# Batch numbers read one unit ahead, first projection weights split early, five heads in halves, operands at 64 bytes

## The reference

```python
x = x + einsum('bct,bcd->bdt', x, W0[cond])                    # 16 maps of 32 x 32
x = x + einsum('bsi,boi->bso', x, W1[cond])                    # 16 maps of 512 x 512
x = x + einsum('bct,bcd->bdt', x, W2[subj]) + bias2[subj]      # 32 maps of 32 x 32
q, k, v = x @ Wq.T, x @ Wk.T, x @ Wv.T                         # 32 query heads, 8 key heads, D = 128
q, k = rope(rmsnorm(q)), rope(rmsnorm(k))
scores = q . [cached keys (16 pages of 32), new keys (32)]     # 4 query heads share a key head
probs = softmax(where(valid, scores * SCALE, -1e30))
x = x + (probs . [cached values, new values]) @ Wo.T
```

## Time and profile before

| | us |
|---|---|
| median of three runs | 2288.32 (2285.64 to 2289.05) |
| profiled execution, its own time | 2286.66 |
| its span in the trace | 2284.8 |

### The profile page before, as it was taken

How to read it: one execution, slowest core, us unless ns; L and a number is a source line. 1 busy time by engine, 2 the same in 40 slices (tenths; PEclk the granted TensorE clock), 3 DMA queues, 4 the chain that set the end, 5 groups by cost and what they waited for, 6 DMA issues and landing times. The chain is left out here.

```text
span 2284.8 us, 52315 instructions
## 1 busy us (share of the span) xinstructions
PE 2231.2 (98%) x16384; PEld 1935.1 (85%) x16384; DVE 1675.9 (73%) x3504; ACT 1297.7 (57%) x2643; POOL 1137.8 (50%) x1218
## 2 busy tenths in 40 slices
PE   7998999999998999999999999999999998999999
PEld 6777777777776999999999999999999997888887
DVE  7860788888887888888888888888888886422221
ACT  6732888888886555555555555555555555311111
POOL 5200354544445777777777777777777773000000
PEclk9999999999998999999999999999999999999999
DMA  6643243444347888888888888888888885543442
GB/s 263 217 107 92 86 127 114 132 134 127 116 140 244 302 303 300 299 297 300 297 290 289 292 297 299 298 301 295 302 300 292 300 298 188 188 139 105 121 129 64
DMA packets 451816, 501.70 MB, mean 220 GB/s; under 512 B 95863, under 2 KB 390775, under 8 KB 443416
## 3 DMA queue, kind: packets, MB, share of 16 engines
q1 hardware_dynamic: 414872, 366.44, 49.3%
q0 software_dynamic: 36864, 134.23, 16.6%
HBM read 408.21 MB, written 92.34 MB: 219 GB/s over the span
## 5 line engine op out<-in xcount | busy, mean ns | idle before, releaser
L1192 POOL TENSOR_TENSOR att_probs<-att_probs,att_inverse 128x512 f32<-128x512 f32 x512 | 535.9, 1047 | 255.0 <-DVE att_inverse L1402 250.7
L1300 ACT ACTIVATE att_probs<-att_probs,att_low 128x544 f32<-128x544 f32 x512 | 383.7, 749 | 472.9 <-DVE att_low L1389 472.9
L1256 PE MATMUL att_o<-att_probs_t,att_values 128*128 128x128 f32 x4096 | 541.0, 275 | 2.1 <-DMA att_values<-L_cond_v_cache,att_v_rows_of 1.8
L1256 PEld LDWEIGHTS att_o<-att_probs_t,att_values 128*128 128x128 f32 x4096 | 497.6, 192 | 2.5 <-DMA att_values<-L_cond_v_cache,att_v_rows_of 2.0
L1389 DVE CUSTOM_DVE_ANT_0 att_probs<-att_score,att_mask,att_batch_cols 128x544 f32<-128x544 f32 x512 | 400.6, 782 | 129.2 <-PE att_score L1218 84.6
L1398 DVE COPY att_probs_t<-att_turn 128x512 f32<-128x512 f32 x512 | 351.0, 686 | 1.2 <-PE att_turn L1233 1.2
L1178 POOL DMA_INDIRECT att_values<-L_cond_v_cache,att_v_rows_of x256 | 270.8, 1058 | 82.5 <-POOL att_v_rows_of L1174 50.1
L1233 PE MATMUL att_turn<-ident,att_probs 128*128 128x128 f32 x2048 | 310.1, 274 | 0.8 <-POOL att_probs L1192 0.4
L1005 POOL TENSOR_TENSOR proj_q_out<-proj_by_cos,proj_by_sin 128x512 f32<-128x512 f32 x128 | 188.6, 1474 | 216.8 <-DVE proj_by_sin L931 216.8
L1233 PEld LDWEIGHTS att_turn<-ident,att_probs 128*128 128x128 f32 x2048 | 241.9, 141 | 36.2 <-issue 8.8
L862 PE MATMUL proj_proj<-x3t_hi,proj_w_hi 128*128 128x512 f32 x640 | 254.6, 398 | 6.7 <-DVE proj_w_lo L916 6.7
(11 more groups left out here) (156 smaller groups left out, 4101.1 us busy)
## 6 DMA issues: line engine op xcount, KB each, us to landing
keys_first<-L_cond_k_cache SPq DMA_DIRECT2D x512, 128.0 KB
att_keys_raw<-L_cond_k_cache SPq DMA_DIRECT2D x512, 128.0 KB
q_t<-proj_q_out SPq DMA_DIRECT2D x32, 1024.0 KB, 5.4
o_t<-att_heads_out SPq DMA_DIRECT2D x64, 512.0 KB, 6.6
out_o_raw<-o_t SPq DMA_DIRECT2D x31, 1024.0 KB, 5.3
queries_first<-q_t SPq DMA_DIRECT2D x32, 512.0 KB
att_queries_raw<-q_t SPq DMA_DIRECT2D x32, 512.0 KB
maps_even<-L_cond_weight SPq DMA_DIRECT2D x8, 1024.0 KB, 12.3
```

The costliest lines, as they stand in the source:

```text
L1192: nc.gpsimd.tensor_tensor(probs[:, k, 0:L], probs[:, k, 0:L], inverse[:, k:k + 1].to_broadcast([P, L]), ALU.mult).then_inc(probs_ready, 1)
L1256: last = nc.tensor.matmul(o_ps[:, at:at + P], values[j][:, t, h * D:(h + 1) * D], probs_t[m % 2][:, t * P:(t + 1) * P], start=(t == 0 and ...
L1300: nc.scalar.activation(probs[:, k, :], probs[:, k, :], ACT.Exp, bias=low[k][:, 0:1], scale=-1.0, accum_out=total[k][:, 0:1]).then_inc(exp_ ...
```

## The change

1. The numbers of unit k + 1 are loaded behind the second fill of unit k (`n % 4 == 1`), into the other of two lists, by VectorE and ScalarE alike; only unit 0's are loaded ahead of its first fill.
2. The first head's projection weights are split in the maps stage: the high parts by ScalarE between the tenth value copy and the sines, the low parts by VectorE at the end of its list. They have a place of their own in high addresses, above what the maps stage uses, that later holds the first batch's keys and then the first heads of the output. SP's waits at the end of the maps stage go; POOL waits for the value stores at the start of the projection, and SP's wait for the stored keys moves from the attention's start to the projection's end.
3. In the attention heads 3 to 7 are taken in halves (`NATIVE = 3`, `ACT_FROM = 3`, `DVE_FROM = 4`). The split parts grow from four heads to five: 384 to 480 columns, and 512 to 640. VectorE's stand in heads 4 to 7 (four) and 0 and 1 (two), the columns in head 3. The first batch's own lists (`FIRST_ACT`, `FIRST_DVE`) are one slot shorter. POOL's order stays.
4. Paddings move the areas named above to multiples of 64 bytes.

```diff
--- before.py
+++ after.py
...
+
+    V_AT = 5120
...
+        a_.sb("to_64_bytes", [P, 8])
...
-        v_out = [odd[:, u * KVD:(u + 1) * KVD].rearrange("p (q h d) -> p q h d", q=GB, d=D) for u in range(U)]
-        pages = odd[:, U * KVD:U * KVD + B * NPP].bitcast(I32).rearrange("p (b n) -> p b n", b=B)
+        v_out = [odd[:, V_AT + u * KVD:V_AT + (u + 1) * KVD].rearrange("p (q h d) -> p q h d", q=GB, d=D) for u in range(U)]
+        pages = odd[:, 0:B * NPP].bitcast(I32).rearrange("p (b n) -> p b n", b=B)
...
-            for u in range(U):
-                sp.wait_ge(v_stored[u], 16 * GB * (G // U))
-            sp.wait_ge(w_nat_loaded, 32)
...
-                if n % 4 == 0:
-                    Q = n // 4 % QUADS
-                    ids[:] = numbers(cond_sb, mybir.EngineType.DVE, Q * QB, QB, CONDS)
+                if n == 0:
+                    unit_numbers(0)
                 may_fill(dve, n)
-                fill(copy, slots_by_dve, BY_DVE, ids, n)
-
-            ids = [None] * QB
+                fill(copy, slots_by_dve, BY_DVE, ids[n // 4 % 2], n)
+
+                if n % 4 == 1 and n // 4 + 1 < UNITS:
+                    unit_numbers(n // 4 + 1)
+
+            ids = [None] * 2
...
+            for m in range(1 + REP):
+                dve.wait_ge(w_hi_ready, m + 1)
+                nc_v.tensor_tensor(w_first_lo[:, m].rearrange("p c e -> p (c e)"), w_nat[:, m, :],
+                                   f32(w_first_hi[:, m]).rearrange("p c e -> p (c e)"), ALU.subtract).then_inc(w_ready, 1)
...
-                    ids[:] = numbers(cond_sb, mybir.EngineType.Activation, Q * QB, QB, CONDS)
+                if n == 0:
+                    unit_numbers(0)
                 may_fill(act, n)
-                fill(copy, slots_by_act, BY_ACT, ids, n)
+                fill(copy, slots_by_act, BY_ACT, ids[n // 4 % 2], n)
+
+                if n % 4 == 1 and n // 4 + 1 < UNITS:
+                    unit_numbers(n // 4 + 1)
...
+
+            act.wait_ge(l1_groups, 4 * UNITS)
+            act.wait_ge(w_nat_loaded, 32)
+            for m in range(1 + REP):
+                copy(w_first_hi[:, m].rearrange("p c e -> p (c e)"), w_nat[:, m, :]).then_inc(w_hi_ready, 1)
...
+            for rc in range(RC):
+                sp.wait_ge(k_stored[rc], 16 * HK)
...
-            for m in range(M):
-                split_weights(0, 0, m, True)
...
+            for u in range(2):
+                pool.wait_ge(v_stored[u], 16 * GB * (G // 2))
...
-    NATIVE = 4
-    ACT_FROM, DVE_FROM = 4, 5
+    NATIVE = 3
+    ACT_FROM, DVE_FROM = 3, 4
...
-    FIRST_ACT = {0: (1, 2), 1: (3, 4), 2: (5,)}
-    FIRST_DVE = {0: (0,), 1: (1, 2), 2: (3, 4), 3: (5,)}
+    FIRST_ACT = {0: (1, 2), 1: (3, 4, 5)}
+    FIRST_DVE = {0: (0,), 1: (1, 2), 2: (3, 4, 5)}
...
-        a_.sb("keys_home", [P, NPP + 1, HK, PSIZE])
-        a_.sb("queries_home", [P, HK, P])
...
+        a_.sb("to_64_bytes", [P, 8])
...
-        o0_hi = a_.sb("o0_hi", [P, REP, CB, S], F32R)
-        o0_lo = a_.sb("o0_lo", [P, REP, CB, S], F32R)
+        o0_hi, o0_lo = o_first
...
-            for rc in range(RC):
-                sp.wait_ge(k_stored[rc], 16 * HK)
...
+                with nc.sbuf_tensor("below_high", [P, BELOW_HIGH], F32):
+                    with (nc.sbuf_tensor("w_hi0", [P, 1 + REP, IC, P], F32R) as w_hi0,
+                          nc.sbuf_tensor("w_lo0", [P, 1 + REP, IC, P], F32R) as w_lo0):
+                        pass
+                    with (nc.sbuf_tensor("keys_first", [P, NPP + 1, HK, PSIZE], F32) as keys_first,
+                          nc.sbuf_tensor("queries_first", [P, HK, P], F32) as queries_first):
+                        pass
+                    with (nc.sbuf_tensor("o0_hi", [P, REP, CB, S], F32R) as o0_hi,
+                          nc.sbuf_tensor("o0_lo", [P, REP, CB, S], F32R) as o0_lo):
+                        pass
                 stage_maps_values(nc, x, w1, cond, subj, w0, w2, b2, wv, wq, wk, table, seqlens, freq, qw, kw, ident,
```

More of the change, by code:

```diff
@@ L51 @@
 ROUND = 1.5 * 2**23
+BELOW_HIGH = 19696
 def rope_frequencies():
@@ L90, in stage_maps_values @@
 def stage_maps_values(nc, x, weight1, cond, subj, w0, w2, bias2, wv, wq, wk, table, seqlens, freq, qw, kw, ident,
-                      early, x3t_hi, x3t_lo, rope, w_nat, stat, v_index, x3_dram, vn_dram):
+                      early, x3t_hi, x3t_lo, rope, w_nat, stat, v_index, x3_dram, vn_dram, w_first, w_sems, v_stored):
     QUADS = G // 4
@@ L117, in stage_maps_values @@
     BY_POOL = (((), (), (), ()), ((), (3,), (), ()))
+    w_first_hi, w_first_lo = w_first
+    w_hi_ready, w_ready = w_sems
+    V_AT = 5120
     with ExitStack() as ctx:
@@ L548, in split_wv, with unit_numbers @@
                      wv_nat[:, part]).then_inc(wv_hi_ready, 1)
+            def unit_numbers(k):
+                ids[k % 2] = numbers(cond_sb, mybir.EngineType.Activation, k % QUADS * QB, QB, CONDS)
             def fill_part(n):
-                if n % 4 == 0:
-                    Q = n // 4 % QUADS
-                    ids[:] = numbers(cond_sb, mybir.EngineType.Activation, Q * QB, QB, CONDS)
+                if n == 0:
+                    unit_numbers(0)
                 may_fill(act, n)
-                fill(copy, slots_by_act, BY_ACT, ids, n)
+                fill(copy, slots_by_act, BY_ACT, ids[n // 4 % 2], n)
+                if n % 4 == 1 and n // 4 + 1 < UNITS:
+                    unit_numbers(n // 4 + 1)
             def keep_values(g):
@@ L718, in stage_projection @@
         SCALE_AT = {9: 0, 12: 1, 14: 2, 16: 3}
-        w_hi, w_lo = [None] * 2, [None] * 2
-        w_hi[0] = a_.sb("w_hi0", [P, M, IC, P], F32R)
-        w_lo[0] = a_.sb("w_lo0", [P, M, IC, P], F32R)
-        a_.sb("rest", [P, (NPP + 1) * HK * PSIZE + HK * P - 2 * M * IC * P])
-        w_hi[1] = a_.sb("w_hi1", [P, M, IC, P], F32R)
-        w_lo[1] = a_.sb("w_lo1", [P, M, IC, P], F32R)
+        w_hi = [w_first[0], a_.sb("w_hi1", [P, M, IC, P], F32R)]
+        w_lo = [w_first[1], a_.sb("w_lo1", [P, M, IC, P], F32R)]
+        w_hi_ready, w_ready = w_sems
         ones = a_.sb("ones", [P, S])
@@ L733, in stage_projection @@
         stat_t = a_.sb("stat_t", [P, CB, S])
+        k_out = [a_.sb(f"k_out{n}", [P, CB, S]) for n in range(RC)]
         q_out = [a_.sb(f"q_out{n}", [P, CB, REP, S]) for n in range(2)]
-        k_out = [a_.sb(f"k_out{n}", [P, CB, S]) for n in range(RC)]
         proj_ps = [a_.ps(f"proj{k}") for k in range(RING)]
@@ L874, in _, with split_weights @@
         def _(act):
-            def split_weights(h, u, m, first=False):
-                if m == 0 and not first:
+            def split_weights(h, u, m):
+                if m == 0:
                     act.wait_ge(w_loaded, h * 32)
@@ L975, in head @@
                         scale_k(h, SCALE_AT[t])
-            for m in range(M):
-                split_weights(0, 0, m)
             dve.wait_ge(first_pages_loaded, 16)
@@ L1674, in program @@
         k_stored = [ctx.enter_context(nc.semaphore(f"k_stored{rc}")) for rc in range(RC)]
+        v_stored = [ctx.enter_context(nc.semaphore(f"v_stored{u}")) for u in range(2)]
+        w_hi_ready = ctx.enter_context(nc.semaphore("w_hi_ready"))
+        w_ready = ctx.enter_context(nc.semaphore("w_ready"))
+        w_sems = (w_hi_ready, w_ready)
         wo_loaded = [ctx.enter_context(nc.semaphore(f"wo_loaded{v}")) for v in range(2)]
```

27 lines of the change are left out of this document (13 added, 14 removed).

## The result

The changed kernel takes 2322.2 us (median of four runs, 2321.6 to 2325.4) against 2287.1 of the kernel before: a ratio of 1.0156, 95% interval 1.0138 to 1.0173, so 35 us slower. Its profiled execution has a span of 2319.7 us against 2284.8.

A forecast was written before the change was run, and what follows sets the result against it. TensorE was taken to bound the kernel, with VectorE and POOL close behind in the attention. From 2286.66 us, gains of 2.6, 3.2, 3.4 and 2.2 and a loss of 30 gave 2305.3, as median 2307; range 2266 to 2324.

The forecast's parts named there:

- the sum: Whole kernel: 2286.66 us profiled, less 2.6, 3.2, 3.4 and 2.2, plus 30, gives 2305.3; 2307 as median.
- the small terms: Outside the attention loop: read-ahead, first weights and alignment together gain 11.4 us.
- The five heads: Attention loop: head 3's slot gains 0.17 us, TensorE stands 0.65; net 0.48 a batch, 30 us lost over 62 batches.
- The step through a batch: Attention: timing from head 3's mask; POOL and VectorE delay each other, head 0's mask 0.86 us late, TensorE stands 0.65.
- rival B: Attention: splits don't lengthen gathers, nothing stands, the slot's 10.5 us is had in full: 2266 us (2262 to 2274); chance 0.30.
- the columns: VectorE in head 3, ahead of its inversion: 0.65 us, delaying POOL's multiply to 2.20 after head 3's mask.
- a wait of some 0.6 ahead of head 1's scores: Attention, sign of being right: TensorE waits some 0.6 us on VectorE's mask there in every batch.
- The rule that was weighed against the sum: Attention: the skill says two-input subtractions don't stall descriptor generation; gathers would then not be lengthened, 2266 instead of 2307 us.
- Numbers one unit ahead: Maps: moving number loads behind the second fill saves TensorE's waits on the adapter copies, 2.6 us (0 to 7.1).
- First weights: Start of the projection: weights split in the maps stage let its first matmul start earlier, 3.2 us gained (0 to 3.2).
- 64 bytes: Alignment: twelve slow output steps gain 3.4 us, the values' 384 matmuls 2.2 (0 if the cause is another).

The follow-up runs named there:

- e13: Changed kernel with splits of one operand plus a running sum, about as long as the two-operand ones, low parts left out: 2272.7 us, 0.9938 of before.
- e4: Changed kernel with POOL's four gathers in heads 3, 5, 7 and the next batch's head 0 instead of 3 to 6: 2330.7 us, 1.0193 of before.
- e10: Changed kernel without the read-ahead of the batch numbers, one trace: the maps take 99.77 us instead of 99.28.
- e7: Changed kernel with the four gathers in heads 3, 4, 6 and 7 instead of 3 to 6: 2328.3 us, 1.0184 of before.
- e8: Changed kernel with gathers in heads 3, 4, 6 and 7 and the columns behind head 2's inversion: 2323.5 us, 1.0165 of before.
- e1: Changed kernel with the attention's old lists (four halved heads), the fifth head's room left empty: 2279.5 us, 0.9966 of before.
- e2: Changed kernel with VectorE's columns moved from head 3 to head 2, ahead of that head's inversion: 2318.8 us, 1.0142 of before.
- e6: Changed kernel with VectorE's columns moved to head 2, behind that head's inversion: 2320.8 us, 1.0153 of before.
- e11: Changed kernel without the padding of the maps stage, one trace: the values take 91.34 us instead of 88.99.

## Why the prediction was right, point by point

**The forecast.** 2322.2 is 15 us above the 2307 and 2 under the range's upper end, so little more would have left it. By the traces the loop lost 11 more than the sum had, the small terms gave 8.6 instead of 11.4, and 2.5 were lost at the attention's start, which was costed at nothing.

**The five heads.** Direction and mechanism held: the attention loses, the batch is 19.2 and not 18.3, splits and gathers lengthen each other. The step through a batch is met closely. From head 3's mask (1346.21) the multiplies of heads 3 to 6 start at 2.33, 5.12, 7.58 and 10.03 (predicted 2.20, 4.97, 7.42, 9.87), the last long split ends at 11.77 (11.62), and head 1's scores start at 12.59 (12.44). The slot of head 3 gained what was said: without the contention (e13) the batch is 18.40, 0.15 under 18.55. That run is also the nearest to rival B, whose gathers are not lengthened: 2272.7 measured, 2266 (2262 to 2274) named.

What was mis-sized is the loss: 0.66 a batch net instead of 0.48, 41 us of the loop instead of 30, and 0.81 of standing instead of 0.65. (The other 2.5 of the attention stand at its start: by the two traces the first batch takes 26.04 instead of 23.32. The prediction costed the first batch's own lists at nothing; what part of it is the clock, at its lower level for 18.6 us of the attention's start after and 10.5 before, was not parted.) The term that was too small is the columns: they took 0.80 (1347.52 to 1348.32) instead of 0.65, because their mask took 0.63 instead of 0.48, and that shifts the whole chain by 0.13 to 0.16. Both masks run beside a gather; the one before starts 0.08 into it, this one 0.60. The sum also had the place wrong: it let TensorE stand only on the masks, first at head 0's scores, and named a wait of some 0.6 ahead of head 1's scores. That sign did not show. In the trace TensorE stands in head 6's slot already, on the turn, whose probabilities come from POOL's multiply, and the standing is spread over four slots: 0.22, 0.36, 0.19 and 0.10 in heads 6, 7, 0 and 1 (by the medians of each, whose sum is not quite the 0.81). (The 0.21 that the sum gives a slot as free is not worked out there; for head 7's, give 1226.45 - 1224.28 - 1.15 - 0.82 = 0.20.)

The better account of the same numbers is a closed loop. A split is held until 0.92 after a multiply's start and then takes 0.65; the gather that started in it ends 0.85 later; the next multiply follows 0.02 behind: 2.44 in all, whatever the start was, and POOL's gathers of heads 4, 5 and 6 do stand 2.45 apart. TensorE's slots there would be 2.10 to 2.20. With 384 columns the loop is 2.35, and the kernel before ran through it once a batch; the change makes it two, with longer splits, and starts it 0.34 later by the columns: 2.92 + 2.45 + 2.45 = 7.82 from the first gather to the last, against 2.58 + 2.21 + 2.35 = 7.14. That is 0.68 more of POOL against slots that got 0.15 shorter: 0.83, of which 0.81 are seen as standing.

**The rule that was weighed against the sum.** The gathers that start in a two-operand split are lengthened, 186 of 256 after, to 1.22 in the mean; with splits of one operand none is (0.99). The Trainium skill, page "SBUF — State Buffer", section "Who interferes with whom", says of this subtraction that it does not stall descriptor generation; the measurement says otherwise, and it decides. Another sentence of that section, that issue order decides who blocks, is borne out by half: in e4 120 gathers were running when a split started, and they took 0.98, but the splits were not held either (0.65 and 0.81, as alone).

**Numbers one unit ahead.** 2.6 was too much: single traces give 0.5 (e10) and 0.8 (before), and neither is clear of the spread of 98.9 to 101.2, so no gain is shown. The waits on line 656 other than the first sum to 10.1 - 6.1 = 4.0 in ten places, and 2.8 of issue: 6.8 in all against 7.1. The loads still cost VectorE and ScalarE their time, and now hold the third fill of a unit instead of the first. The prediction gave this as the reason for its lower bound.

**First weights.** 3.2 predicted, 7.13 - 3.90 = 3.23 measured (3.90 to 3.93 in all traces with the change), the first product at 220.24 against the 221 named. (That date is partly luck: it counted on 2.6 from the maps, which did not come, and the 1.40 of the clock made up for it.) It starts 0.60 after SP's last store (217.87 + 1.77 = 219.64), for which the prediction had 0.63:

```profile
220.24 0.49 PE L883 MATMUL proj_proj<-x3t_hi,w_hi 128*128 128x512 f32 x1 [3.52 <-POOL proj_ones L1025]
```

The projection then takes 1.6 longer, which the prediction did not have. The traces put it in the heads whose weights lie in the new place, every second one: their 240 products take 60.98 instead of 60.53 in all traces with the change, and four times 0.45 is 1.8. Why products out of that place take some 2 ns longer is open. The clock plays a part beside it: it is low over the first microseconds of the projection (0.53 to 0.62 before, 0.57 after). In e4, e7 and e8, where it is at 1.00 there, the same projection takes 484.78, and the attention starts 7.04 behind it, as before: so the 0.9 is not the wait for the stored keys, which these runs have too.

**64 bytes.** The values gained 2.35 by it (2.2 predicted). In the output two steps (timeline as in the earlier trace rows) take 2073.38 - 2062.50 = 10.88 and 2084.36 - 2073.38 = 10.98:

```profile
2062.50 0.39 PE L1568 MATMUL out_y<-out_wot_hi,out_o_hi 128*128 128x512 f32 x1
...
2073.38 0.39 PE L1568 MATMUL out_y<-out_wot_hi,o_hi 128*128 128x512 f32 x1
...
2084.36 0.39 PE L1568 MATMUL out_y<-out_wot_hi,out_o_hi 128*128 128x512 f32 x1
```

So the slow steps kept 0.11 over the others (medians 10.99 and 10.88) although the change puts all operands at multiples of 64; the first steps of the chunks, 10.91 before, take 10.99 too, and the stage gained 2.46 instead of 3.4. All steps of 10.99 read the heads (`o_hi`, `o_lo`) that lie in the same new place as the weights above, and 0.11 in 48 products is again some 2 ns each.

Together the parts that show are 3.2 - 1.8 + 2.35 + 2.46 = 6.2 us; e1 measures 7.0 against the kernel before, with 4.6 to 11.0 as its interval.

## What to carry to other kernels

Before you give VectorE longer two-operand work beside a POOL chain, write down the loop that the two form (hold, work, gather's rest) and compare its period with the bounding engine's slot: an average share of 76% and 50% says nothing about it. A step that only started the loop earlier, or moved one member of it, changed next to nothing here (19.13 and 19.18 against 19.21 in e2 and e6); taking away the second operand did. Taking gathers out of the heads that split freed those heads too (e4), but the values then came late; taking the splits out of the heads that gather was not tried. Look for a stand in every wait of the bounding engine on the loop's members, the turn on POOL as well as the scores on VectorE.

## What was not expected of the hardware

- A gather that starts in a two-operand subtraction ends 0.85 to 0.87 us after the subtraction, however early it was issued (184 of 186 after, all 126 before). One that is running when the subtraction starts is not touched (0.98 in 120 cases of e4), nor is the subtraction.
- The columns' mask, a multiply-compare with one operand in SBUF and scalars, is held by POOL too: 0.48 alone, 1.12 beside a multiply, and beside a gather 0.49 when it starts 0.08 into it (before) and 0.63 when it starts 0.60 into it (after). The Trainium skill, page "SBUF — State Buffer", section "Who interferes with whom", lists such instructions among those that can take the shared ports; the rows beside a multiply agree.
- Operands 32 bytes beside a multiple of 64 cost TensorE's products 2.35 us in 384 of 512 columns, 6 ns each (e11; the clock was at 1.00 in both traces).
